# State space layer: the feed-forward half starts one loop step earlier, its first chunk through one PSUM bank

## The chip, the core and the metric

The kernel runs on one core of a Trainium2 chip. A core has a matrix engine (TensorE, here PE), a vector engine (DVE), an activation engine (ACT) and a general engine (POOL), each working through its own queue of instructions in order; they wait for each other on semaphores. Matrix products land in PSUM, which has banks of 512 fp32 numbers per partition. The metric is the device time of one execution in microseconds (us), lower is better. A measurement of this kernel moves by a few tenths of a per cent from run to run: the three runs below lie from 1214.46 to 1218.0 us.

## What is computed

Four transformer-like layers run over 64 images of 36 tokens with 128 features. The change touches the second layer alone: a Mamba-2 state space block followed by a feed-forward block, cut here to what matters.

```python
t = tgt + _mamba2(tgt, ...)           # conv, silu, decay matrix, gated output, W_out
t = _layernorm(t, n1_g, n1_b)
h = jax.nn.gelu(t @ ffn_w1 + ffn_b1, approximate=False) @ ffn_w2 + ffn_b2
return _layernorm(t + h, n3_g, n3_b)  # added to h of the layer below, then normalised again
```

In the state space block `exp` makes the decays between tokens and `tanh` makes the two silu functions; the feed-forward block uses `gelu`. So ACT needs one table of functions in the first block and another in the second.

## The kernel before

**Tiling.** Tokens lie in G = 22 groups of P = 108 (three images of 36). The feed-forward block takes them in nb = 6 chunks (CHUNKS): five of four groups, one of two. In `state_phase`, after some preparation, every engine runs the same loop `for t in range(last)`, whose step t holds a piece of several groups at once, the later stages of earlier groups: `group(t, k)` is group t - k, or nothing.

**The state space stages of a group g**, by step: at t = g DVE writes `ss_cum` (L2646). At t = g+1 PE makes the decay sums (L2465), turns the conv output (L2473, L2474, bank 3) and makes the gate z (L2476, bank 1); ACT takes `exp` (L2560, `ss_L`), copies bank 3 (L2565, `ss_xc`) and takes `tanh` of z (L2568); DVE waits for `ss_xc` at L2658. At g+2 PE multiplies by the values (L2490), DVE makes `ss_ys` and `ss_yz` (L2677, L2679), ACT squares it (L2581). At g+3 PE turns `ss_yz` (L2481), ACT copies it to `ss_yT` (L2572), PE applies W_out (L2498) and DVE adds and takes statistics (L2686 to L2692). At g+4 the group is normalised (DVE L2670, POOL L2381 to L2385). At g+5 PE turns it (L2504) and ACT copies it to `XP` (L2584); at g+6 DVE writes the low part of `XP` (L2653), for the split products. While tiles of the convolution are left (t up to 19), PE and ACT also work on one of them in each step, in bank 2.

**The feed-forward stages**, class `FeedForward`: at every step t from `first_fed` on, each engine appends to its loop step the feed-forward step s = t - `first_fed`. There are `steps` = nb + 4 = 10 of them. With chunk n:
- s = n: `up(n)` on PE: four groups of three products into `hid_bank(i)`, i = 4n + c (L2144); ACT takes `gelu` of each into `fs_hid` (L2216).
- s = n+1: `down(n)` on PE, 16 products (L2160).
- s = n+2: DVE adds it to `T` (L2248) and takes statistics, POOL makes scale and shift (L2117 to L2122), ACT normalises `T`, as the last thing of its step (L2199).
- s = n+3: DVE (L2256, L2259) adds into `H` and takes statistics, POOL again.
- s = n+4: ACT normalises into `XN` (L2199), PE turns it (L2172), ACT copies (L2221), PE makes the routing products (L2182).

Before, `first_fed` = G = 22, so `up(0)` stands in step 22, where the last group (21) has its first PE stage, and `last` is 32. `hid_bank` goes round three banks: 2, 3 and the first of `quad_bank`. Banks 3 and that one are used by the loop until group 21 has been read out of them at step 22; therefore `up(0)` waits for `xc_ready` = G and `decay` = G. `up` lets PE run two `gelu` behind: before product group i it waits for `hid_ready` = i - 2.

**What sets the order** is the order in which the code is written, for each engine, and the semaphores. There is no scheduler. When the loop is over, `logits` (L2266) ends the phase, and the next phase starts behind a barrier.

Of the kernel before, what the change touches and what calls it, by code (L numbers as in the profile page):

```python
# [10 lines left out]
ALU = mybir.AluOpType  # L11
# [9 lines left out]
P = TB * S  # L21
G = -(-BATCH // TB)
# [30 lines left out]
def at_least(eng, sem, value):  # L53

    if not isinstance(value, int) or value > 0:
        eng.wait_ge(sem, value)
# [1999 lines left out]
class FeedForward:  # L2056
# [6 lines left out]
    def __init__(self, nc, m, ctx, sem, io, rows, layer):  # L2063
        sb = lambda s, shape, dt=F32: ctx.enter_context(nc.sbuf_tensor(f"fs_{s}", shape, dt))
        self.m, self.io, self.rows, self.layer = m, io, rows, layer
        self.nb, hid_n = len(CHUNKS), 4 * 128
        self.steps = self.nb + 4
        self.w1_loaded, self.loaded = sem("fs_w1_loaded"), sem("fs_loaded")
        self.w_high, self.w_split = sem("fs_w_high"), sem("fs_w_split")
        self.moved = sem("fs_moved")  # L2070
        self.hid_psum, self.hid_ready, self.y_psum, self.t_sum = sem("fs_hid_psum"), sem("fs_hid_ready"), sem("fs_y_psum"), sem("fs_t_sum")
        self.t_stats, self.t_steps, self.t_rstd = sem("fs_t_stats"), sem("fs_t_steps"), sem("fs_t_rstd")
        self.t_normed, self.t_scaled = sem("fs_t_normed"), sem("fs_t_scaled")
        self.h_sum, self.h_stats, self.h_steps, self.h_rstd = sem("fs_h_sum"), sem("fs_h_stats"), sem("fs_h_steps"), sem("fs_h_rstd")
        self.xn_ready, self.xt_psum, self.xt_ready = sem("fs_xn_ready"), sem("fs_xt_psum"), sem("fs_xt_ready")
        self.lg_psum, self.lg_ready = sem("fs_lg_psum"), sem("fs_lg_ready")
        self.rows_stored = m.kept.enter_context(nc.semaphore("fs_rows_stored"))
        self.w1s, self.w2s = sb("w1s", [128, hid_n]), sb("w2s", [128, hid_n])
        self.b1s, self.wr = sb("b1s", [128, 4]), sb("wr", [128, 8])
        self.w1p = sb("w1p", [128, 2, hid_n], F32R)  # L2080
        self.hid = sb("hid", [128, 2, 4, QUAD * P])
        self.t_bn, self.h_bn = sb("t_bn", [P, G, 6]), sb("h_bn", [P, G, 6])
        self.t_mv, self.h_mv = sb("t_mv", [P, G, 2]), sb("h_mv", [P, G, 2])
        self.t_scale, self.h_scale = sb("t_scale", [P, G]), sb("h_scale", [P, G])
        self.t_shift, self.h_shift = sb("t_shift", [P, G]), sb("h_shift", [P, G])
        self.wide = lambda row, k: m.row(row).unsqueeze(1).broadcast_to([P, k, D])
        self.hid_bank = lambda i: (m.bank[2], m.bank[3], m.quad_bank[:, 0, :])[i % 3]
        self.y_bank = lambda n: (m.bank[1], m.quad_bank[:, 1, :])[n % 2]
        self.turn_bank, self.lg_bank = m.bank[0], m.quad_bank[:, 2, :]

# [40 lines left out]
    def up(self, pe, n):  # L2131
        m, layer = self.m, self.layer
        c0, k = CHUNKS[n]
        pe.wait_ge(layer.t_split, c0 + k)
        if n == 0:
            pe.wait_ge(self.w_split, 1)
            pe.wait_ge(layer.cv_ready, 4 * self.nb)
            pe.wait_ge(layer.xc_ready, G)
            pe.wait_ge(layer.decay, G)
        for c in range(4):  # L2140
            i = n * 4 + c
            at_least(pe, self.hid_ready, i - 2)
            for a, b in PARTS:
                mm = pe.matmul(self.hid_bank(i)[:, 0:k * P], self.w1p[:, a, c * 128:(c + 1) * 128],  # L2144
                               m.XP[:, b, c0 * P:(c0 + k) * P], start=((a, b) == PARTS[0]), stop=((a, b) == PARTS[-1]))
            mm.then_inc(self.hid_psum, 1)
# [124 lines left out]
def state_phase(nc, m, io, taps, rows):  # L2271
# [2 lines left out]


    nb = len(CHUNKS)
    first_fed = G
    with ExitStack() as ctx:
        sem = ctx.enter_context(semaphores(nc, m, "ss"))
        sb = lambda s, shape, dt=F32: ctx.enter_context(nc.sbuf_tensor(f"ss_{s}", shape, dt))  # L2280
# [16 lines left out]
        t_psum, t_ready, t_split = sem("t_psum"), sem("t_ready"), sem("t_split")  # L2297
# [291 lines left out]
        def _(dve):  # L2589
# [43 lines left out]
            for k in (15, 13, 11, 9, 7, 5, 3):  # L2633
# [4 lines left out]
            then(dve.scalar_tensor_tensor(out=m.DTA[:, :].rearrange("p (g e) -> p g e", e=8), in0=m.DT[:, :].rearrange("p (g e) -> p g e", e=8),  # L2638
                                          scalar=-1.0, in1=a_exp[:, :].unsqueeze(1).broadcast_to([P, G, 8]), op0=ALU.mult, op1=ALU.mult))

            for t in range(last):
                if t and (at := tile(t - 1)) is not None:
                    gated(*at)
# [4 lines left out]
                if t == 0:  # L2648
                    for c in range(4):
                        gated(0, c)  # L2650
                if (g := group(t, 6)) is not None:
                    dve.wait_ge(t_ready, g + 1)
                    dve.tensor_tensor(m.XP[:, 1, g * P:(g + 1) * P], t_bank[:, 0:P], m.XP[:, 0, g * P:(g + 1) * P],  # L2653
                                      ALU.subtract).then_inc(t_split, 1)
                if (g := group(t, 1)) is not None:
                    dve.wait_ge(xc_ready, g + 1)
                    at_least(dve, mix_ready, g)
# [35 lines left out]
                if G + 1 <= t < G + 4:  # L2693
                    for n in range(2):
                        feed.move(dve, 2 * (t - G - 1) + n)
                if t >= first_fed:
                    feed.vector(dve, t - first_fed)
            feed.logits(dve)
# [712 lines left out]
```

## Time and profile before

| | us |
|---|---|
| median of 3 runs | 1216.21 |
| lowest, highest | 1214.46, 1218.0 |
| the profiled execution, its own time | 1212.65 |
| its span in the trace | 1210.9 |
| the stretch from step 22 on PE to the last routing product's sum | 511.4 to 576.9 |

The profiled execution is 3.56 us shorter than the median of the runs, and 1.75 us of it lie outside the span. Times in the trace are counted from the start of the span. In a timeline a row begins with the start and the duration of a run of like instructions; what stands in brackets is how long the engine sat idle before it and who released it. Each step of the loop can be found by its rows: `ss_cum` opens PE's part, `XP` ends ACT's part of the loop, `fs_w1p` and `fs_w2s` are `up` and `down`.

### The profile page before, as it was taken

What the parts mean: (1) busy time and instruction counts of PE and PEld (TensorE: products, weight loads), DVE (VectorE), ACT (ScalarE), POOL (GpSimd) and SP (SyncE); (2) the same over time, 40 slices, a digit from 0 to 9 for tenths busy, and PEclk for the clock granted to TensorE, in tenths of its full rate; (3) what the DMA queues carried; (4) which work ended last, traced back from release to release, by engine and by line L of the source; (5) the groups of instructions that cost most, each with busy time, mean ns of one, the idle gap of its engine ahead of it and who ended that gap; (6) DMA issues with size and microseconds to landing.
All of it is one profiled execution on the core that took longest, in us unless ns stands there. A gap on an engine that the chain in (4) does not pass through costs nothing. (4 is left out here: it accounts for less than half of the span.)

```text
span 1210.9 us, 29369 instructions
## 1 busy us (share of the span) xinstructions
PE 1083.4 (89%) x8538; PEld 906.9 (75%) x8538; DVE 926.1 (76%) x2799; ACT 856.6 (71%) x2831; POOL 527.4 (44%) x869
## 2 busy tenths in 40 slices
PE   8899999999998999887397689997899899869996
PEld 7788868888887888786387577786688688657884
DVE  5588868999875889856675797885899788755774
ACT  5598979888885555456253578886788499746995
POOL 0489984445104278865252643223432111034552
PEclk9999989999999999998599799999999999959998
DMA  7300003312110000001522200000443000024441
GB/s 299 98 2 3 2 2 94 97 66 66 61 41 24 1 2 1 2 1 41 199 64 48 68 9 6 7 2 1 133 119 109 21 2 2 3 82 123 130 129 44
DMA packets 50824, 66.68 MB, mean 55 GB/s; under 512 B 8100, under 2 KB 30904, under 8 KB 50552
## 3 DMA queue, kind: packets, MB, share of 16 engines
q1 hardware_dynamic: 44552, 53.39, 14.5%
q0 software_dynamic: 4432, 6.59, 2.1%
q10 hardware_dynamic: 1696, 4.98, 1.0%
q8 instruction: 65, 1.06, 0.4%
q14 instruction: 79, 0.65, 0.2%
HBM read 58.32 MB, written 6.71 MB: 54 GB/s over the span
## 5 line engine op out<-in xcount | busy, mean ns | idle before, releaser
L545 DVE TENSOR_TENSOR f_parts<-T,f_parts 128x512 fp32r<-128x512 f32 (+1 forms) x240 | 185.1, 810 | 21.6 <-ACT f_parts L529 19.7
L521 ACT ACTIVATE T<-quad_bank,f_b1s 128x512 f32<-128x512 f32 (+1 forms) x240 | 150.7, 648 | 47.7 <-PE quad_bank L492 39.0
L492 PE MATMUL quad_bank<-XP,f_wp 128*128 128x512 f32 (+1 forms) x720 | 167.9, 378 | 0.2 <-ACT T L521 0.2
L492 PEld LDWEIGHTS quad_bank<-XP,f_wp 128*128 128x128 f32 x720 | 127.2, 191 | 25.6 <-issue 0.9
L529 ACT ACTIVATE f_parts<-T 128x512 fp32r<-128x512 f32 (+1 forms) x240 | 132.2, 591 | 0.0
L1015 ACT ACTIVATE a_late<-quad_bank,a_shift 108x108 f32<-108x108 f32 x352 | 119.0, 361 | 2.7 <-DVE a_shift L1101 2.6
L505 PE MATMUL bank<-f_parts,f_wp 128*128 128x512 f32 (+1 forms) x480 | 113.7, 372 | 4.6 <-DVE XT L554 2.0
L505 PEld LDWEIGHTS bank<-f_parts,f_wp 128*128 128x128 f32 x480 | 84.0, 188 | 22.4 <-DVE XT L554 2.6
L434 POOL TENSOR_TENSOR f_wp<-f_ws,const 128x512 fp32r<-128x512 f32 (+1 forms) x32 | 34.0, 1064 | 120.5 <-DMA f_ws<-in_f_w 56.0
L1015 ACT ACTIVATION_READ_ACCUMULATOR a_late<-quad_bank,a_shift 108x1 f32 x352 | 76.7, 218 | 0.0
L821 POOL TENSOR_TENSOR a_ve<-a_mv,const 108x1 f32<-108x1 f32 x44 | 8.4, 191 | 148.4 <-DVE a_mv L1158 148.4
L1471 ACT ACTIVATE a_late<-a_masked,a_shift 108x108 f32<-108x108 f32 x176 | 65.1, 374 | 0.8 <-DVE a_shift L1555 0.7
L510 PE MATMUL bank<-f_parts,f_wp 128*128 128x512 f32 (+1 forms) x240 | 63.1, 370 | 0.6 <-DVE f_parts L545 0.6
L3108 ACT ACTIVATE a_E<-quad_bank,a_shift 108x108 f32<-108x108 f32 x184 | 61.9, 353 | 0.7 <-DVE a_shift L3149 0.4
L1097 DVE TENSOR_REDUCE a_mx<-quad_bank 108x4 f32<-108x432 f32 x88 | 53.0, 603 | 9.4 <-PE quad_bank L898 8.3
L1937 ACT ACTIVATE f_hid<-quad_bank,f_b1t 128x128 f32<-128x128 f32 x100 | 28.8, 368 | 41.2 <-PE quad_bank L1905 41.2
L2428 PE MATMUL bank<-ss_xp,ss_wtp 128*128 128x432 f32 (+1 forms) x264 | 55.5, 360 | 2.4 <-ACT ss_th L2527 1.3
L898 PE MATMUL quad_bank<-a_qk 19*108 19x108 f32 x704 | 55.4, 273 | 2.5 <-ACT a_late L1015 1.2
L898 PEld LDWEIGHTS quad_bank<-a_qk 19*108 19x108 f32 x704 | 40.8, 168 | 16.1 <-issue 5.3
L1007 ACT ACTIVATE a_late<-bank 108x432 f32<-108x432 f32 x88 | 48.0, 545 | 4.9 <-PE bank L873 3.2
L574 DVE SCALAR_TENSOR_TENSOR a_late<-bank,f_b2s,a_late 128x512 f32<-128x512 f32 (+1 forms) x70 | 48.1, 687 | 4.2 <-DMA a_late<-f_gates 3.0
L2428 PEld LDWEIGHTS bank<-ss_xp,ss_wtp 128*128 128x128 f32 x264 | 45.5, 191 | 6.1 <-issue 2.9
(484 smaller groups left out, 3119.8 us busy)
## 6 DMA issues: line engine op xcount, KB each, us to landing
a_late<-f_gates SPq DMA_DIRECT2D x64, 256.0 KB, 3.3
a_wqk<-in_a_wqk SPq DMA_DIRECT2D x24, 256.0 KB, 2.5
f_ws<-in_f_w SPq DMA_DIRECT2D x16, 256.0 KB, 4.0
pats<-in_patches SPq DMA_DIRECT2D x5, 648.0 KB, 10.7
pats<-in_patches ACTq DMA_DIRECT2D x5, 648.0 KB, 15.8
a_late<-f_gates SPq DMA_DIRECT2D x16, 128.0 KB, 3.7
f_w1a<-in_f_w SPq DMA_DIRECT2D x1, 2048.0 KB, 10.7
f_w2a<-in_f_w SPq DMA_DIRECT2D x1, 2048.0 KB, 15.5
```

What stands on the lines that cost most here:

```text
L492: mm = pe.matmul(self.m.quad_bank[:, q % 4, 0:w], self.wp[0][:, e % 2, a, c * 128:(c + 1) * 128], self.xp[:, b, t0:t0 + w], start=((a, b) ...
L505: pe.matmul(self.y_bank(i)[:, 0:w], self.wp[1][:, e % 2, a, c * 128:(c + 1) * 128], self.hi[:, q % self.ring, 0:w], start=(c == 0 and a == ...
L510: mm = pe.matmul(self.y_bank(i)[:, 0:w], self.wp[1][:, e % 2, 0, c * 128:(c + 1) * 128], self.lo[:, q % self.ring, 0:w], start=False, stop ...
L521: act.activation(self.full[:, q % 4, 0:w], self.m.quad_bank[:, q % 4, 0:w], self.func, bias=self.b1s[:, e * self.chunks + c:e * self.chunk ...
L529: act.activation(self.hi[:, q % self.ring, 0:w], self.full[:, q % 4, 0:w], ACT.Copy).then_inc(self.hid_high, 1)
L545: dve.tensor_tensor(self.lo[:, q % self.ring, 0:w], self.full[:, q % 4, 0:w], self.hi[:, q % self.ring, 0:w], ALU.subtract).then_inc(self. ...
L898: mm = pe.matmul(sbank[0:P, b, tile * P:(tile + 1) * P], qk[row * b:row * b + used, q, tile, :], qk[row * b:row * b + used, q, tiles + til ...
L1015: e = act.activation(E[:, q, n, :], scores[:, n // tiles, n % tiles, :], ACT.Exp, scale=w.scale, bias=shift[:, q, n:n + 1], accum_out=tota ...
L1097: dve.tensor_reduce(top.rearrange("p (b s) -> p b s", s=tiles), scores[:, banks * half:banks * (half + 1), :, :], AX, ALU.max).then_inc(ma ...
L1471: e = act.activation(E[:, g % 2, n, :], masked[:, half, i, :], ACT.Exp, scale=-1.0, bias=shift[:, g % 2, n:n + 1], accum_out=total[:, g % ...
L2428: mm = pe.matmul(conv_bank(s, c)[:, 0:k * P], wtp[:, a, tap, c * 128:(c + 1) * 128], xp[:, s % 2, b, 0:k * TB, tap:tap + S], start=(tap == ...
L3108: e = act.activation(E[:, u, n, :], scores[:, n // tiles, n % tiles, :], ACT.Exp, scale=scale, bias=shift[:, u, n:n + 1], accum_out=total[ ...
```

## The change

- `first_fed` becomes G - 1 = 21. Every feed-forward step stands one loop step earlier, and `last` becomes 31: the loop has one step fewer.
- `up(0)` now stands in step 21, when banks 3 and `quad_bank` 0 are still wanted by group 21. So its four product groups all go to bank 2, the bank of the convolution, free since step 19: `hid_bank(i)` is bank 2 for i up to 3, and each group waits for the `gelu` of the one before (`hid_ready` = i).
- The wait for `xc_ready` and `decay` moves from `up(0)` to `up(1)`.
- `up(5)` needs the low part of `XP` of group 21, which was written at step 27, and now would come after its reader; it is written at step G + 4 = 26, just before DVE's feed-forward step (`turned_low`).

```diff
-        self.hid_bank = lambda i: (m.bank[2], m.bank[3], m.quad_bank[:, 0, :])[i % 3]
+        self.hid_bank = lambda i: (m.bank[2], m.bank[3], m.quad_bank[:, 0, :])[i % 3 if i > 3 else 0]
...
         if n == 0:
             pe.wait_ge(self.w_split, 1)
             pe.wait_ge(layer.cv_ready, 4 * self.nb)
+        if n == 1:
             pe.wait_ge(layer.xc_ready, G)
             pe.wait_ge(layer.decay, G)
         for c in range(4):
             i = n * 4 + c
-            at_least(pe, self.hid_ready, i - 2)
+            at_least(pe, self.hid_ready, i if n == 0 else i - 2)
...
-    first_fed = G
+    first_fed = G - 1
...
+            def turned_low(g):
+                dve.wait_ge(t_ready, g + 1)
+                dve.tensor_tensor(m.XP[:, 1, g * P:(g + 1) * P], t_bank[:, 0:P], m.XP[:, 0, g * P:(g + 1) * P],
+                                  ALU.subtract).then_inc(t_split, 1)
+
...
-                if (g := group(t, 6)) is not None:
-                    dve.wait_ge(t_ready, g + 1)
-                    dve.tensor_tensor(m.XP[:, 1, g * P:(g + 1) * P], t_bank[:, 0:P], m.XP[:, 0, g * P:(g + 1) * P],
-                                      ALU.subtract).then_inc(t_split, 1)
+                if (g := group(t, 6)) is not None and g < G - 1:
+                    turned_low(g)
...
+                if t == G + 4:
+                    turned_low(G - 1)
                 if t >= first_fed:
                     feed.vector(dve, t - first_fed)
```

No instruction of the computation is added or taken away; the instructions of the changed kernel stand one line lower than before (L2145 for L2144 and so on), from the feed-forward class on.

**PE, from the last row of step 21.** Before, the last group's first stages follow, and then `up(0)` over three banks:

```order
L2504 MATMUL quad_bank<-const,ss_tt 128x108
L2465 MATMUL quad_bank<-ss_cum,const 108x432
L2473 MATMUL bank3<-const,ss_sx 108x128 x2
L2474 MATMUL bank3<-ss_sx 108x108
L2476 MATMUL bank1<-ss_win,XT 108x256
L2481 MATMUL bank0<-const,ss_yz 128x108 x2
L2490 MATMUL quad_bank<-ss_xdt,ss_M 108x64 x4
L2498 MATMUL quad_bank<-ss_wout,ss_yT 108x128 x2
L2504 MATMUL quad_bank<-const,ss_tt 128x108
L2144 MATMUL bank2<-XP,fs_w1p 128x432 x3
L2144 MATMUL bank3<-XP,fs_w1p 128x432 x3
L2144 MATMUL quad_bank<-XP,fs_w1p 128x432 x3
```

Now `up(0)` comes first, twelve products into bank 2, and `up(1)` stands where `up(0)` stood:

```order
L2505 MATMUL quad_bank<-const,ss_tt 128x108
L2145 MATMUL bank2<-XP,fs_w1p 128x432 x12
L2466 MATMUL quad_bank<-ss_cum,const 108x432
L2474 MATMUL bank3<-const,ss_sx 108x128 x2
L2475 MATMUL bank3<-ss_sx 108x108
L2477 MATMUL bank1<-ss_win,XT 108x256
L2482 MATMUL bank0<-const,ss_yz 128x108 x2
L2491 MATMUL quad_bank<-ss_xdt,ss_M 108x64 x4
L2499 MATMUL quad_bank<-ss_wout,ss_yT 108x128 x2
L2505 MATMUL quad_bank<-const,ss_tt 128x108
L2145 MATMUL bank3<-XP,fs_w1p 128x432 x3
```

What moved is `up(0)`, ahead of the eight rows of step 22.

**ACT, from the last row of step 21.** Before, the last `exp` and `tanh` are over when `gelu` begins, and there is one load of a function table:

```order
L2584 ACTIVATE XP<-quad_bank 128x108
L2560 ACTIVATE ss_L<-quad_bank 108x432
L2565 ACTIVATE ss_xc<-bank3 108x364
L2568 ACTIVATE ss_zs<-bank1 108x256
L2572 ACTIVATE ss_yT<-bank0 128x216
L2581 ACTIVATE ss_sq,ss_ssq<-ss_yz 108x256
L2584 ACTIVATE XP<-quad_bank 128x108
L2216 ACT_TABLE_LOAD
L2216 ACTIVATE fs_hid<-bank2,fs_b1s 128x432
L2216 ACTIVATE fs_hid<-bank3,fs_b1s 128x432
```

Now `gelu` of chunk 0 stands ahead of them, and there are three loads:

```order
L2585 ACTIVATE XP<-quad_bank 128x108
L2217 ACT_TABLE_LOAD
L2217 ACTIVATE fs_hid<-bank2,fs_b1s 128x432 x4
L2561 ACT_TABLE_LOAD
L2561 ACTIVATE ss_L<-quad_bank 108x432
L2566 ACTIVATE ss_xc<-bank3 108x364
L2569 ACTIVATE ss_zs<-bank1 108x256
L2573 ACTIVATE ss_yT<-bank0 128x216
L2582 ACTIVATE ss_sq,ss_ssq<-ss_yz 108x256
L2585 ACTIVATE XP<-quad_bank 128x108
L2217 ACT_TABLE_LOAD
L2217 ACTIVATE fs_hid<-bank3,fs_b1s 128x432
```

What moved is the chunk's `gelu`, and a load stands on either side of the loop's part of step 22.

**ACT at step 24**, where the last group's `ss_yT` is copied. Before, the copy comes before the first normalisation of `T` (L2199):

```order
L2572 ACTIVATE ss_yT<-bank0 128x216
L2584 ACTIVATE XP<-quad_bank 128x108
L2216 ACTIVATE fs_hid<-quad_bank,fs_b1s 128x432
L2216 ACTIVATE fs_hid<-bank2,fs_b1s 128x432
L2216 ACTIVATE fs_hid<-bank3,fs_b1s 128x432
L2216 ACTIVATE fs_hid<-quad_bank,fs_b1s 128x432
L2199 ACTIVATE T<-T,fs_t_shift,fs_t_scale 108x128 x4
```

Now it comes behind it:

```order
L2217 ACTIVATE fs_hid<-quad_bank,fs_b1s 128x432
L2217 ACTIVATE fs_hid<-bank2,fs_b1s 128x432
L2217 ACTIVATE fs_hid<-bank3,fs_b1s 128x432
L2217 ACTIVATE fs_hid<-quad_bank,fs_b1s 128x432
L2200 ACTIVATE T<-T,fs_t_shift,fs_t_scale 108x128 x4
L2573 ACTIVATE ss_yT<-bank0 128x216
L2585 ACTIVATE XP<-quad_bank 128x108
```

The normalisation of the first chunk has moved from the end of step 24 to the end of step 23, ahead of the copy.

## Rows read from the trace of the kernel before

**Rows 1.** The page: the span.

```profile
span 1210.9 us, 29369 instructions
```

**Rows 2.** Stretches: start:end, length, busy time of each engine, granted clock (PEclk).

```profile
526.70:558.50 31.80, 29.42 (x237) 28.08 (x236) 19.24 (x78) 20.11 (x48) 17.45 (x34) 1.00 0.06 15
558.50:577.00 18.50, 10.24 (x67) 8.88 (x65) 10.08 (x41) 10.46 (x26) 9.59 (x23) 0.71 0.16 42
```

**Rows 3.** The timeline of PE, steps 21 to 25 and on: start, duration, operation.

```profile
511.31 0.26 PE L2504 MATMUL quad_bank<-const,ss_tt 108*128 108x108 f32 x1
511.40 1.51 PE L2465 MATMUL quad_bank<-ss_cum,const 108*108 108x432 f32 x2
...
513.14 0.56 PE L2474 MATMUL bank<-ss_sx 128*108 128x108 f32 x2
...
516.05 1.43 PE L2144 MATMUL bank<-XP,fs_w1p 128*128 128x432 f32 x6
...
520.59 0.86 PE L2144 MATMUL bank<-XP,fs_w1p 128*128 128x432 f32 x3 [2.51 <-ACT fs_hid L2216]
...
523.57 1.43 PE L2144 MATMUL bank<-XP,fs_w1p 128*128 128x432 f32 x3
...
526.74 3.65 PE L2160 MATMUL bank<-fs_w2s,fs_hid 128*108 128x128 f32 x32
...
531.02 0.69 PE L2498 MATMUL quad_bank<-ss_wout,ss_yT 128*108 128x128 f32 x4 [0.44 <-ACT ss_yT L2572]
...
534.02 3.65 PE L2160 MATMUL quad_bank<-fs_w2s,fs_hid 128*108 128x128 f32 x32
...
541.58 3.65 PE L2160 MATMUL bank<-fs_w2s,fs_hid 128*108 128x128 f32 x32
...
548.79 3.66 PE L2160 MATMUL quad_bank<-fs_w2s,fs_hid 128*108 128x128 f32 x32
...
554.88 3.66 PE L2160 MATMUL bank<-fs_w2s,fs_hid 128*108 128x128 f32 x32
```

**Rows 4.** The timeline of ACT around the table load, and of its first normalisations.

```profile
513.86 0.24 ACT L2584 ACTIVATE XP<-quad_bank 128x108 fp32r<-128x108 f32 x1
...
514.41 0.48 ACT L2565 ACTIVATE ss_xc<-bank 108x364 f32<-108x364 f32 x1
...
518.63 1.28 ACT L2216 ACT_TABLE_LOAD   x1
...
520.94 0.62 ACT L2216 ACTIVATE fs_hid<-quad_bank,fs_b1s 128x432 f32<-128x432 f32 x1
...
538.54 1.65 ACT L2199 ACTIVATE T<-T,fs_t_shift,fs_t_scale 108x128 f32<-108x128 f32 x4 [3.69 <-POOL fs_t_shift L2122]
...
547.07 0.60 ACT L2216 ACTIVATE fs_hid<-bank,fs_b1s 128x432 f32<-128x432 f32 x1
```

**Rows 5.** The timeline of DVE at step 22, step 25 and the end of the phase.

```profile
514.92 0.27 DVE L2658 TENSOR_TENSOR ss_cbm<-ss_xc,const 108x108 f32<-108x108 f32 x1 [0.49 <-ACT ss_xc L2565]
...
524.61 1.26 DVE L2230 TENSOR_TENSOR H<-H,rows 108x512 f32<-108x512 f32 x2
...
533.79 0.68 DVE L2248 TENSOR_TENSOR T<-T,bank 108x512 f32<-108x512 f32 x1
...
545.35 0.69 DVE L2248 TENSOR_TENSOR T<-T,bank 108x512 f32<-108x512 f32 x1 [2.12 <-PE bank L2160]
...
549.98 0.23 DVE L2653 TENSOR_TENSOR XP<-quad_bank,XP 128x108 fp32r<-128x108 f32 x1
...
576.56 0.34 DVE L2266 TENSOR_TENSOR LG<-quad_bank,rows 108x176 f32<-108x176 f32 x1 [5.52 <-PE quad_bank L2182]
```

**Rows 6.** Stretches of PE alone, 1 us long: busy time, granted clock.

```profile
510.00:511.00 1.00, 0.22 (x2) 1.00 0.00 0
...
512.00:513.00 1.00, 1.00 (x4) 0.50 0.00 0
```

**Rows 7.** Who waited for whom on PE from 511 to 577 us: total, times, longest.

```profile
PE bank L2144 <- ACT fs_hid L2216: 4.5, 3, 2.5
```

## Prediction

> **What bounds the kernel now.** I read the stretches first, then PE's waits, then the timelines. From `down(0)` to the end of `down(4)` PE is busy for 29.42 of 31.80 us at a granted clock of 1.00 [rows 2]: this stretch is PE's own work, nearly back to back. What follows `down(4)` is a chain of sums, normalisations and turns in which PE is busy 10.24 of 18.50 us [rows 2]; it ends with `logits` at 576.56 [rows 5], and nothing of the next phase can start before. So the end of the phase is the start of `down(4)`, 554.88, plus a tail of 21.7 us whose order the change leaves alone. The reader needs five landmarks on PE, the starts of `down(0)` to `down(4)`: 526.74, 534.02, 541.58, 548.79, 554.88 [rows 3]. There is one visible thing to win: within `up(0)` PE sat idle 2.51 us for the first `gelu` [rows 3], out of 4.5 us of such waits in the phase [rows 7]. There is one fact against it: ACT is not free for a `gelu` before its last work of step 21 ends at 513.86 + 0.24 = 514.10, and the table load costs 1.28 us more [rows 4]. One step fewer is worth nothing in itself, since no instruction goes away; it is worth what idle time it removes.
>
> **Step 21: `up(0)` through one bank.** PE reaches it at 511.3 [rows 3] and runs its first group at once. `gelu` 0 can start at 514.10 + 1.28 = 515.4 and takes 0.62 [rows 4]: done at 516.0. Each of the other three groups then waits for the `gelu` before it. A group takes 0.86 us at the full clock and 1.43 at half [rows 3], both clocks occurring, 1.00 and 0.50 [rows 6], a `gelu` 0.62, and a hand-over 0.05 (`ss_xc` ends at 514.89 and its reader starts at 514.92 [rows 4, 5]; I round up). That is 1.6 or 2.15 us a round. The clock fell to 0.50 in 512 to 513 after a microsecond in which PE was busy only 0.22 [rows 6]; here PE idles over 3 us before the second group, so I take the full clock for one round and half for two. The last group starts at 519.8 and PE is free at 521.0. At the full clock throughout it would be 519.9. Before, the same PE was already in step 22 at 511.40 [rows 3].
>
> **Step 22: two more table loads.** ACT ends the fourth `gelu` at 521.9. `exp` and `tanh` of group 21 need the other table: 1.28 us, then `ss_L` (0.4) and `ss_xc` (0.48 [rows 4]), done at 524.1 where it was 514.9. PE had its input ready at 521.0 + 2.3 = 523.3 (511.40 to 513.14 + 0.56 [rows 3]), so ACT decides. DVE's part of the step shifts by 9.2 us with it. From DVE's reader of `ss_xc` to the start of ACT's load it was 514.92 to 518.63 [rows 4, 5], 3.7 us; I take 3.5, as the shift leaves POOL time to be ready. So the third load begins at 527.6, the first `gelu` of chunk 1 ends at 529.5, and the fourth group of `up(1)`, which waits for it, lets `down(0)` start at 530.4 instead of 526.74: **+3.7**. The two loads (2.6 us) are inside this sum, one fully exposed, the other behind PE's groups.
>
> The Trainium skill (ScalarE: Activation LUTs, What ACT_TABLE_LOAD costs) puts every switch of set at about 1.28 us of load and 1.38 us of drain; its section Table sets: the hidden batching unit asks to batch calls by set, which speaks against this change. The trace agrees on the load and not on the drain. By the page's price the two added loads would cost some 2.8 us more, and the forecast would be +12.7.
>
> **Step 23.** From `down(0)` to `down(1)` took 7.3 us [rows 3]. Now the value product of group 21 lies in it too; I take 7.6: `down(1)` at 538.0, **+4.0** in all.
>
> **Step 24: the last group behind the first normalisation.** DVE can add chunk 0 into `T` only after its own part of step 23, which waits for the output product of group 20 (ends near 535.9), then statistics (0.9) and two `H` additions (1.2 [rows 5]): 538.0. From there to ACT's normalisation took 533.79 to 538.54, 4.75 us [rows 4, 5]: it starts at 542.8 and ends at 544.4. Before, ACT had copied `ss_yT` of group 21 ahead of it, and PE waited 0.44 us [rows 3]. Now the copy is behind it, and PE, which is there at 541.9, starts the output product only at 544.75: 2.8 us idle. From that product to the next `down` it took 3.0 us [rows 3]; `down(2)` starts at 547.8, **+6.2**.
>
> **Step 25: DVE late, then ACT.** DVE gets group 21's sum at 545.4, and after the same 2.1 us adds chunk 1 into `T` at 547.5. That addition to the low part of `XP` took 545.35 to 549.98 [rows 5], 4.6 us: 552.2. PE needs it to turn group 20 and is free at 551.3: 1.1 us idle. ACT normalises `T` at 547.5 + 4.75 = 552.2, then `XN` (1.65 each [rows 4]), so its first `gelu` of chunk 4 comes at 555.6 instead of 547.07 [rows 4]. `down(3)` came 1.72 us behind that: 557.3, **+8.5**.
>
> **Step 26: the moved low part.** PE turns group 21 at 561.5, ACT copies it (0.24), DVE makes the low part (0.23), and `up(5)`, which before stood right behind, waits for both, about 0.9 us in all. ACT's normalisation of `XN` can only begin after that copy, and `gelu` behind it costs another 0.5. `down(4)`: 6.1 + 1.4 us after `down(3)`, 564.8, **+9.9**. The tail hangs on it unchanged. DVE waits for the copy of group 21 at its `turned_low`, with chunk 3's sum queued behind; that is inside the same 9.9. POOL's queue is only later with DVE's, and SP stores `XN` chunk by chunk behind it.
>
> **The sum.** Against the profiled execution 1212.65 + 9.9 = 1222.6 (its span 1210.9 [rows 1] + 9.9 = 1220.8). Against the median of the runs, 3.56 us higher: 1216.21 + 9.9 = 1226.1, or 0.8% slower.
>
> **Bounds of what the trace doesn't show.** The clock after so many short waits: at full clock throughout, 1.1 less (8.8). If half the clock also catches `down(0)`, its 3.65 us double: 3.5 more; another 2 if it catches a later chunk. In the tail PE did idle and the clock was 0.71 on average [rows 2], so this can happen. A later wait can turn out shorter than worked out: the 2.8 us of step 24 can vanish if DVE and POOL serve chunk 0 faster, and steps 25 and 26 can be absorbed in part. Then about +4 is left.
>
> **Rivals.**
> 1. *The later waits are absorbed.* Steps 21 to 23 cost what is worked out, but PE takes the rest up: +4, 1220. For it: ACT and DVE have gaps. Against it: the copy of `ss_yT` stands behind the normalisation in ACT's own queue.
> 2. *Half the clock in PE's long stretch*: +9.9 + 3.5 to 5.5, 1229.6 to 1231.6. For it: the clock fell after idling [rows 6]. Against it: after the 2.51 us of idling it was back before `down(0)` (1.00 in 526.70 to 558.50 [rows 2]). The Trainium skill (TensorE: Matmul & The Clock Gate, What's actually happening) has the clock depend on how busy PE has been of late, which bears this rival out in kind.
> 3. *Not slower: the moved chunk fills PE.* `up(0)` runs where PE idled, so the 2.51 us go, and PE keeps the full clock through step 22, which at 0.50 took 4.65 us (511.40 to 516.05 [rows 3, 6]) and would take some 3.2: together -4, 1212.2. It decides by ACT: `gelu` 0 would have to end about when PE's second group could start, 512.4, and ACT is busy until 514.10 without the load. Only if DVE, not PE, set the pace of all that follows would the delay be hidden.
> 4. *The page's drain*: +12.7, 1228.9.
> 5. *Nothing happens*, the delays of steps 21 and 22 cancelled by fewer waits later (4.5 us in all to be had [rows 7]): within 0.3%.
>
> **Chances.** Forecast as worked out (+7.5 to +12.5) 0.55; rival 1 0.17; rival 2 0.12; rival 3 0.04; rival 4 0.03; rival 5 0.09. A measurement can tell 0.3%, 3.6 us, from no change. Rival 1 sits just above this bound, and I count a third of it (0.05) as no change. Faster 0.04, same 0.14, slower 0.82. The range takes in rivals 1, 2 and 4: 1219.5 to 1232.
>
> **What would show it.** In the trace of the changed kernel: three table loads between 514 and 529 us; `up(0)` with three waits of PE for `gelu`; PE idle over 2 us before the output product of group 21, released by the copy of `ss_yT`; the five landmarks at 530.4, 538.0, 547.8, 557.3, 564.8; `logits` at 586.5. The prediction is wrong if `down(0)` starts by 527, or if the landmarks stop drifting after `down(1)`, which is rival 1, or if the granted clock falls below 1.00 in that stretch, rival 2.

## The result

The changed kernel is slower: 1227.22 us (median of 4 runs, 1225.51 to 1228.42) against 1216.87 us for the kernel before in the same comparison. The ratio is 1.0094, with a 95% interval of 1.0069 to 1.0119. The forecast was 1226.1 us. In a second comparison, 1227.73 against 1215.47 us, the ratio was 1.0096 (1.0069 to 1.0124). So the change costs 0.9 to 1.0%; the medians differ by 10.4 and 12.3 us, and the two intervals together reach from 8.4 to 15 us.

To compare traces I measure one stretch, called D: from PE's turn of group 16, the last thing that both kernels do in the same place, to the start of `logits`. Before, D is 576.56 - 511.31 = 65.25 [rows 3, 5].

### The profile page after: what moved, and what is told of

It is laid out like the page before. It is cut to its first block and busy times, and to the rows that moved or that the text cites. A ratio compares the mean times of both kernels' runs of the same rounds, so it can differ in the third digit from the quotient of the medians.

```text
span 1226.0 us, 29371 instructions
## 1 busy us (share of the span) xinstructions
PE 1090.5 (89%) x8538; PEld 912.4 (74%) x8538; DVE 924.9 (75%) x2799; ACT 858.4 (70%) x2833; POOL 521.5 (43%) x869
## 5 line engine op out<-in xcount | busy, mean ns | idle before, releaser
L505 PE MATMUL bank<-f_parts,f_wp 128*128 128x512 f32 (+1 forms) x480 | 115.6, 377 | 4.0 <-DVE a_late L574 1.7
L505 PEld LDWEIGHTS bank<-f_parts,f_wp 128*128 128x128 f32 x480 | 85.1, 190 | 22.1 <-DVE a_late L574 2.6
L434 POOL TENSOR_TENSOR f_wp<-f_ws,const 128x512 fp32r<-128x512 f32 (+1 forms) x32 | 31.3, 978 | 125.8 <-DMA f_ws<-in_f_w 64.7
L510 PE MATMUL bank<-f_parts,f_wp 128*128 128x512 f32 (+1 forms) x240 | 64.2, 376 | 0.1
L510 PEld LDWEIGHTS bank<-f_parts,f_wp 128*128 128x128 f32 x240 | 43.7, 191 | 8.9 <-DVE f_parts L545 0.7
```

The source lines that it names most:

```text
L505: pe.matmul(self.y_bank(i)[:, 0:w], self.wp[1][:, e % 2, a, c * 128:(c + 1) * 128], self.hi[:, q % self.ring, 0:w], start=(c == 0 and a == ...
L510: mm = pe.matmul(self.y_bank(i)[:, 0:w], self.wp[1][:, e % 2, 0, c * 128:(c + 1) * 128], self.lo[:, q % self.ring, 0:w], start=False, stop ...
```

## The profile after

The page of the changed kernel, its span and the busy time of its engines:

```profile
span 1226.0 us, 29371 instructions
PE 1090.5 (89%) x8538; PEld 912.4 (74%) x8538; DVE 924.9 (75%) x2799; ACT 858.4 (70%) x2833; POOL 521.5 (43%) x869
```

As many products as before, and two more ACT instructions: the table loads. The timeline of PE in the changed kernel (start, duration, operation, idle before and releaser), which answers to [rows 3]:

```profile
511.73 0.26 PE L2505 MATMUL quad_bank<-const,ss_tt 108*128 108x108 f32 x1
511.76 0.83 PE L2145 MATMUL bank<-XP,fs_w1p 128*128 128x432 f32 x3
516.51 1.45 PE L2145 MATMUL bank<-XP,fs_w1p 128*128 128x432 f32 x3 [3.91 <-ACT fs_hid L2217]
518.67 1.45 PE L2145 MATMUL bank<-XP,fs_w1p 128*128 128x432 f32 x3 [0.71 <-ACT fs_hid L2217]
...
530.38 0.90 PE L2145 MATMUL bank<-XP,fs_w1p 128*128 128x432 f32 x3 [2.11 <-ACT fs_hid L2217]
531.08 5.30 PE L2161 MATMUL bank<-fs_w2s,fs_hid 128*108 128x128 f32 x32
...
540.17 3.65 PE L2161 MATMUL quad_bank<-fs_w2s,fs_hid 128*108 128x128 f32 x32
...
546.01 0.69 PE L2499 MATMUL quad_bank<-ss_wout,ss_yT 128*108 128x128 f32 x4 [2.00 <-ACT ss_yT L2573]
...
549.01 3.65 PE L2161 MATMUL bank<-fs_w2s,fs_hid 128*108 128x128 f32 x32
553.74 0.28 PE L2505 MATMUL quad_bank<-const,ss_tt 108*128 108x108 f32 x1 [1.07 <-issue]
...
558.38 1.45 PE L2145 MATMUL bank<-XP,fs_w1p 128*128 128x432 f32 x3 [2.40 <-ACT fs_hid L2217]
...
560.34 4.36 PE L2161 MATMUL quad_bank<-fs_w2s,fs_hid 128*108 128x128 f32 x32
...
566.17 0.59 PE L2145 MATMUL quad_bank<-XP,fs_w1p 128*128 128x216 f32 x3 [0.65 <-DVE XP L2644]
...
568.53 3.66 PE L2161 MATMUL bank<-fs_w2s,fs_hid 128*108 128x128 f32 x32
```

`up(0)` has its three waits, the last group's output product waits 2.00 us for the copy behind the normalisation, and the moved low part holds `up(5)` back for 0.65 us. ACT in the same stretch, answering to [rows 4]:

```profile
514.28 0.24 ACT L2585 ACTIVATE XP<-quad_bank 128x108 fp32r<-128x108 f32 x1
514.54 1.28 ACT L2217 ACT_TABLE_LOAD   x1
515.84 0.62 ACT L2217 ACTIVATE fs_hid<-bank,fs_b1s 128x432 f32<-128x432 f32 x1
...
522.95 1.28 ACT L2561 ACT_TABLE_LOAD   x1
...
528.41 1.28 ACT L2217 ACT_TABLE_LOAD   x1
...
544.08 1.65 ACT L2200 ACTIVATE T<-T,fs_t_shift,fs_t_scale 108x128 f32<-108x128 f32 x4 [3.09 <-POOL fs_t_shift L2122]
545.63 0.33 ACT L2573 ACTIVATE ss_yT<-bank 128x216 f32<-128x216 f32 x1
```

And two rows of DVE. The first had waited for `ss_xc` of group 21, which ACT makes only behind the chunk's four `gelu` and the second table load; the other row ends the phase:

```profile
525.17 0.27 DVE L2662 TENSOR_TENSOR ss_cbm<-ss_xc,const 108x108 f32<-108x108 f32 x1 [10.32 <-ACT ss_xc L2566]
...
590.67 0.34 DVE L2267 TENSOR_TENSOR LG<-quad_bank,rows 108x176 f32<-108x176 f32 x1 [5.98 <-PE quad_bank L2183]
```

D is now 590.67 - 511.73 = 78.94: 13.7 us more than before, where the forecast had 9.9. The granted clock tells most of why. Stretches of the changed kernel, as in [rows 2]:

```profile
514.00:524.00 10.00, 6.07 (x14) 3.79 (x15) 0.73 (x4) 5.33 (x9) 2.56 (x7) 0.50 0.00 0
524.00:531.00 7.00, 4.89 (x32) 4.27 (x32) 3.69 (x12) 4.87 (x12) 3.39 (x8) 0.98 0.00 0
531.00:534.00 3.00, 3.00 (x16) 2.96 (x15) 0.05 (x1) 0.94 (x2) 1.36 (x3) 0.51 0.03 5
```

PE ran at 1.2 GHz (0.50) for ten microseconds around `up(0)`, and again for the first three of `down(0)`, which took 5.30 us where it took 3.65 before.

Who waited for whom on PE, the changed kernel, 511 to 590 us, answering to [rows 7]:

```profile
PE bank L2145 <- ACT fs_hid L2217: 9.9, 5, 3.9
...
PE quad_bank L2499 <- ACT ss_yT L2573: 2.8, 2, 2.0
```

The change was to remove some of PE's waits for `gelu`, 4.5 us in all before [rows 7]; they have grown to 9.9.

## The experiments

Each was compared with the kernel before on the chip on which it ran. "Before, again", "changed, again", "one table" and "one bank" ran on one chip, "copy first", "kept busy", "changed, mended" and "early load" on a second, and the two with "and busy" on a third, so two ratios of different chips are compared with less certainty than two of one. D is from one profiled execution each. The columns "down" have the start of that product group counted from the turn of group 16. Several causes act on the same microseconds (a round of `up(0)` is longer both by its wait and by the clock), so the shares found below overlap and can't be added up.

| kernel | ratio to before (95%) | D | down(0) | down(2) | down(4) |
|---|---|---|---|---|---|
| before | | 65.25 | 15.43 | 30.27 | 43.57 |
| before, again | 1.0005 (0.9988 to 1.0022) | 64.36 | 14.09 | 28.93 | 42.23 |
| changed | 1.0094 (1.0069 to 1.0119) | 78.94 | 19.35 | 37.28 | 56.80 |
| changed, again | 1.0096 (1.0069 to 1.0124) | 78.53 | 19.35 | 37.30 | 56.85 |
| one table | 1.0069 (1.0042 to 1.0096) | 76.40 | 17.20 | 35.15 | 54.73 |
| one bank | 1.0038 (1.0022 to 1.0055) | 70.19 | 20.38 | 35.21 | 48.52 |
| copy first | 1.0095 (1.0070 to 1.0119) | 75.34 | 19.35 | 34.05 | 53.66 |
| kept busy | 1.0075 (1.0054 to 1.0096) | 73.46 | 17.58 | 35.29 | 51.78 |
| changed, mended | 1.0069 (1.0046 to 1.0093) | 70.25 | 15.92 | 30.64 | 48.57 |
| mended and busy | 1.0040 (1.0023 to 1.0058) | 70.72 | 14.72 | 29.43 | 49.05 |
| early load | 0.9983 (0.9966 to 1.0000) | 62.51 | 12.71 | 27.54 | 40.84 |
| early and busy | 0.9986 (0.9971 to 1.0001) | 62.51 | 12.71 | 27.54 | 40.83 |

### Both kernels once more

> The kernel before, unchanged, once more. Measure for all runs: D, from PE's turn of group 16 (the last row of step 21's loop part; 511.31 in the first profile) to the start of logits (576.56): 65.3 us before, 590.67 - 511.73 = 78.9 after, so +13.7 inside the phase in one profile each, while the medians differ by 10.4. Theory 1 (the phase is repeatable, and the rest of the gap lies in other phases of single executions): D = 65.3 within 0.5, ratio 1.000 within 0.002. Rival (the phase itself varies by microseconds with the clock): D differs by more than 1.

> The changed kernel, unchanged, once more. Theory 1: D = 78.9 within 0.5 and down(0) again at half clock in part (5.3 us against 3.65). Rival (how much of the phase runs at half clock is chance): D between 75.2, the 9.9 forecast, and 79, with down(0) at 3.65 us when it is short. Ratio to before 1.008 to 1.012 by both.

The changed kernel repeated itself to 0.4 us, half clock in `down(0)` (5.32 us) included. The kernel before did so less well: D is 0.9 us shorter, which meets neither the 0.5 us of theory 1 nor the more than 1 of its rival. The table shows where: `down(0)` comes 1.34 us sooner, and of this the stretch behind `down(4)` gives 0.45 back. The 1.34 us lie in step 23. Stretches of PE alone, the first profile and then the repeat:

```profile
522.00:523.00 1.00, 1.00 (x7) 0.50 0.00 0
523.00:524.00 1.00, 1.00 (x6) 0.50 0.00 0
```

```profile
512.00:514.00 2.00, 1.56 (x12) 1.00 0.00 0
...
522.00:524.00 2.00, 2.00 (x14) 1.00 0.01 4
```

The first profile was also at 0.50 from 512 to 513 [rows 6], where the repeat has 1.00, but this cost nothing: from `ss_cum` to `up(0)` it took 4.65 us in the one and 4.60 in the other, since at the full clock PE waits there for ACT and DVE instead (0.83 and 0.33 us). In the tail it was the repeat that fell sooner:

```profile
559.17 3.12 PE L2160 MATMUL quad_bank<-fs_w2s,fs_hid 128*108 128x128 f32 x16
```

This `down(5)` took 1.91 us in the first profile. So when the clock falls, in a phase that idles now and then, differs from execution to execution, and moved D by about 1 us here. The cost of the change in D is 13.7 us against the first profile and 14.2 between the two repeats. Both lie within the intervals of the ratios (8.4 to 15 us). Other phases of a span also differ by a microsecond or two between profiles, which is why I judge single terms by D.

### One table

Edit: chunk 0 takes a function that lies in the same table as `exp`.

```diff
-                act.activation(self.hid[:, s % 2, c, 0:k * P], self.hid_bank(i)[:, 0:k * P], ACT.Gelu,
+                act.activation(self.hid[:, s % 2, c, 0:k * P], self.hid_bank(i)[:, 0:k * P], ACT.Gelu if s else ACT.Tanh,
```

> The changed kernel with tanh instead of gelu for chunk 0 of the feed-forward block (this part of the computation is replaced): chunk 0 needs no other function table, so one load of three is left. Theory 1 (the two added loads are exposed on PE's path in steps 21 and 22): first activation of chunk 0 1.28 us sooner, ss_xc of group 21 2.6 us sooner, down(0) 2.4 to 2.6 sooner, D = 76.3, ratio to before 1.0065 to 1.0085. Rival A (the loads hide behind PE's groups): D = 78 to 79. Rival B (the clock is what costs, and shorter idling keeps it up): D below 74.5.

D is 76.40, 2.1 to 2.5 us less than in the two profiles of the changed kernel, and `down(0)` is 2.15 us sooner. ACT in this kernel:

```profile
511.39 0.24 ACT L2585 ACTIVATE XP<-quad_bank 128x108 fp32r<-128x108 f32 x1
511.53 0.61 ACT L2217 ACTIVATE fs_hid<-bank,fs_b1s 128x432 f32<-128x432 f32 x1
513.09 0.62 ACT L2217 ACTIVATE fs_hid<-bank,fs_b1s 128x432 f32<-128x432 f32 x1 [0.94 <-PE bank L2145]
...
517.41 0.62 ACT L2217 ACTIVATE fs_hid<-bank,fs_b1s 128x432 f32<-128x432 f32 x1 [1.54 <-PE bank L2145]
518.85 0.53 ACT L2561 ACTIVATE ss_L<-quad_bank 108x432 f32<-108x432 f32 x1 [0.82 <-PE quad_bank L2466]
```

And PE's second group, which ran at the full clock here and at half in the changed kernel (1.45 us):

```profile
512.20 0.85 PE L2145 MATMUL bank<-XP,fs_w1p 128*128 128x432 f32 x3 [2.49 <-ACT fs_hid L2217]
```

Counted from the turn of group 16, the first activation of chunk 0 starts 1.42 us sooner than in the changed kernel: this is the first load with the gaps beside it, fully exposed. The fourth starts 2.02 us sooner, since one of the three rounds took 1.56 us and not 2.16: that is the clock. `ss_L` starts 2.51 us sooner, so the second load was worth only 0.5 us more: without it ACT waits 0.82 us for PE's `ss_cum` product, a wait that the load had covered. Of these 2.51 us `down(0)` keeps 2.15, where 2.4 to 2.6 were expected. So at `ss_L` the two added loads make 1.9 us, and the clock 0.6. Theory 1 is right in D (76.3 expected) and in the ratio, but it took both loads for exposed, and the second was so for less than half. Rival A, with D at 78 to 79, falls, though it holds in part for the second load. Rival B falls too, with D below 74.5: only one round came back to the full clock, and `down(0)` took 5.32 us as before.

### One bank

Edit: the kernel before, `first_fed` 22, with these lines of the change alone.

```diff
-        self.hid_bank = lambda i: (m.bank[2], m.bank[3], m.quad_bank[:, 0, :])[i % 3]
+        self.hid_bank = lambda i: (m.bank[2], m.bank[3], m.quad_bank[:, 0, :])[i % 3 if i > 3 else 0]
...
-            at_least(pe, self.hid_ready, i - 2)
+            at_least(pe, self.hid_ready, i if n == 0 else i - 2)
```

> The kernel before with one part of the change alone: first_fed stays 22, one table load, but the four groups of up(0) go through bank 2, each waiting for the gelu before it. Theory 1 (serial groups cost PE a round of 1.6 to 2.15 us for each of the two that used to run ahead): the last group of up(0) starts 3.2 to 4.3 us later than 520.59, down(0) 3 to 4 us later, D = 68.5 to 69.5, ratio 1.002 to 1.004. Rival (ACT, not PE, sets the pace here, since it ends the four gelus at 522.1 anyway): D = 66 to 67.

The ratio, 1.0038, is as theory 1 had it; D is 70.19, more than the 68.5 to 69.5 that it had: 4.9 us over the first profile of before, 5.8 over the repeat. PE in this kernel:

```profile
516.48 0.83 PE L2144 MATMUL bank<-XP,fs_w1p 128*128 128x432 f32 x3
521.05 1.45 PE L2144 MATMUL bank<-XP,fs_w1p 128*128 128x432 f32 x3 [3.74 <-ACT fs_hid L2216]
523.22 1.45 PE L2144 MATMUL bank<-XP,fs_w1p 128*128 128x432 f32 x3 [0.71 <-ACT fs_hid L2216]
525.38 1.45 PE L2144 MATMUL bank<-XP,fs_w1p 128*128 128x432 f32 x3 [0.71 <-ACT fs_hid L2216]
```

All three rounds run at half clock, 2.16 us each, and so does step 23 behind them (its clock is 0.50 up to 530 us). From the turn of group 16 to the last group it is 4.3 us more than before, the upper end of theory 1; what is beyond it is step 23 at half clock. One bank instead of three costs by itself over a third of what the change costs, before anything is moved. This share has the half clock that the waits bring with them in it, so it overlaps with the clock's share below.

### The copy first

Edit: at the end of step 23 ACT makes the copy of group 21 before it normalises `T`, and no longer at the start of step 24.

```diff
+        if s == 2:
+            self.before_norm()
         if 0 <= s - 2 < nb:
             self.norm(act, s - 2, m.T[0:P, :], m.T[0:P, :], self.t_scale, self.t_shift, self.t_rstd, self.t_normed)
...
-                if (g := group(t, 3)) is not None:
+                if (g := group(t, 3)) is not None and g < G - 1:
+                    turned_copy(g)
```

> The changed kernel with one pair of ACT's instructions exchanged: the copy of ss_yT of group 21 stands ahead of the first normalisation of T, at the end of step 23. D is the time from PE's turn of group 16 to the start of logits (65.3 before, 78.9 after). Theory 1 (the 2.00 us that PE idles before the output product of group 21 come from this order and pass on to the end): PE idle there 0.4, down(2) 1.6 sooner, D = 77.0 to 77.5. Rival (the chain of sums and normalisations on DVE, POOL and ACT sets steps 24 and 25 anyway): down(2) sooner, D = 78.5 to 79.

PE's idle time at the output product is 0.44 us instead of 2.00, and from `down(1)` to `down(2)` it is 7.27 us instead of 8.84, 1.6 less. PE in this kernel:

```profile
532.71 3.65 PE L2161 MATMUL bank<-fs_w2s,fs_hid 128*108 128x128 f32 x32
...
544.42 0.69 PE L2501 MATMUL quad_bank<-ss_wout,ss_yT 128*108 128x128 f32 x4 [0.44 <-ACT ss_yT L2562]
```

D fell by 3.2 to 3.6, more than the 1.4 to 1.9 expected, because `down(0)`, which starts at the same 19.35, ran at the full clock this time (3.65 us and not 5.30). Up to there the two kernels run the same instructions, so this second part isn't the edit's but the execution's. The time does not show the gain: the ratio is 1.0095. The span fell by nothing either, since in this execution the rest of the program took longer (638.0 us behind `logits` against 635.3 and 635.8 in the changed kernel's two). So the order's 1.6 us is seen in the trace and not confirmed by the times, which can't tell it.

### PE kept busy

Edit: products on constants, whose results nothing reads, in the gaps.

```diff
             mm.then_inc(self.hid_psum, 1)
+            if n == 0 and c < 3:
+                at_least(pe, layer.decay, G - 1)
+                keep_busy(pe, m, m.quad_bank[:, 0, :], (9, 1, 1)[c])
+            if n == 1 and c == 2:
+                keep_busy(pe, m, m.bank[0], 4)
```

> The changed kernel with products on constants, whose results are not used, in PE's gaps: nine after the first group of up(0), one after the second and third, four in up(1) ahead of its last group. Theory 2 (part of the cost is half clock after idling: the groups of up(0) took 1.45 us instead of 0.83, down(0) 5.30 instead of 3.65): granted clock 1.00 from 514 to 536, groups 0.85, down(0) 3.65, D = 75.5 to 76.5. Rival (ACT's loads and gelus cover it): D = 78 to 79.

D is 73.46, 5.1 to 5.5 us less than the changed kernel, where 2.4 to 3.4 were expected, and the ratio is 1.0075. PE in this kernel, and two stretches of PE alone:

```profile
512.00 4.05 PE L66 MATMUL quad_bank<-const 128*128 128x256 f32 x18
...
528.85 3.65 PE L2166 MATMUL bank<-fs_w2s,fs_hid 128*108 128x128 f32 x32
```

```profile
514.00:518.00 4.00, 3.71 (x17) 1.00 0.00 0
...
542.00:546.00 4.00, 3.87 (x16) 0.67 0.01 4
```

The clock stays at 1.00 to 542 us, the rounds take 1.57 us instead of 2.16, and `down(0)` takes 3.65. Two counts agree on what the half clock is worth in the changed kernel. Between the starts of `down(0)` to `down(4)` in the table, the filler gains 1.8 us up to `down(0)` and 5.0 up to `down(4)`. And the changed kernel's own rows give the same: 1.8 in three rounds, 1.65 in `down(0)`, 0.9 in the group before `down(3)` and the turns with it, 0.7 in `down(3)`. On the way the filler kernel lost 1.4 us in step 24, where PE idled 2.01 us for the copy as before and the clock then fell (0.67 in 542 to 546), and won this back in step 25, whose waits for DVE and ACT shrank by it. So about 5 of the 14 us in D are the clock's. The times agree in direction only: 1.0075 and 1.0094 to 1.0096 have intervals that overlap, and are from two chips.

What remains is 9.1 us against the repeat of before, and up to `down(4)` 8.2 us against the first profile and 9.6 against the repeat. The forecast's sum for the full clock was 8.8.

### Three repairs, and with the filler as well

Edits: "changed, mended" has the exchanged copy, and in steps 21 and 22 a `gelu` of one column of constants where ACT idles, which brings the table load with it (the lines of this second edit are below). "Mended and busy" has also five, one and one filler products between the groups of `up(0)`.

```diff
+                if t in (G - 1, G):
+                    act.activation(early[:, t % 2:t % 2 + 1], m.eps[0:P, :], ACT.Gelu)
                 if (at := tile(t)) is not None:
                     evict(*at)
```

> The changed kernel with the exchanged copy of ss_yT and with gelu of one column of constants in steps 21 and 22, in ACT's idle time, so that two of three table loads lie there. Theory 1: first gelu of chunk 0 at the end of step 21's XP copy (1.3 sooner), first gelu of chunk 1 1.3 sooner, PE's idle time at the output product 0.4: D = 74 to 75, still some 9 us over before. Rival (the step sooner wins once the loads are out of the way): D at or below 65.3.

> The changed kernel with the exchanged copy, the two early table loads and products on constants (results not used) between the groups of up(0), five after the first and one after the second and third. With the loads, the order and the clock out of the way only the structure is left: four serial groups in step 21 and the later steps on DVE, ACT and POOL. Theory 1: granted clock 1.00 in steps 21 and 22, D = 68.0 to 69.3 against 64.4 of the repeat of the kernel before, which had the full clock as well; ratio to before 1.003 to 1.007. Rival (the three repairs together bring the change to even): D = 65.5 or less, ratio 1.000 or less.

Both are still slower than the kernel before, by 0.7% and 0.4%, with both intervals above 1. So the rivals, that the step sooner would then be worth something or break even, both fall. In D they are at 70.25 and 70.72, where 74 to 75 and 68.0 to 69.3 were expected. The first did better than expected, since `down(0)` and `down(3)` kept the full clock. The second gained another 1.2 us up to `down(2)` and lost it in `down(3)`, which fell to half clock behind a wait of PE for `gelu` of chunk 4; its expectation had the clock out of the way. For "mended and busy", who waited for whom on PE (total, times, longest), and the stretch of PE alone in which the clock fell:

```profile
PE bank L2145 <- ACT fs_hid L2220: 4.0, 5, 2.4
...
PE quad_bank L2511 <- issue: 1.1, 1, 1.1
PE quad_bank L2145 <- DVE XP L2655: 0.7, 1, 0.7
```

```profile
552.00:556.00 4.00, 4.00 (x24) 0.57 0.15 42
```

The three waits that no repair touched (2.4 us for `gelu` behind two normalisations, 1.1 for DVE's low part of group 19, 0.7 for the low part of group 21) are 4.2 us together; the kernel before had 0.6 us of wait in the same place. The trace names no releaser for the 1.1 us ("issue"). That it is the low part of group 19 I take from the semaphore in the code, and from the changed kernel's trace, where this low part ends at 553.64 and PE's turn starts at 553.74. `down(2)` of "mended and busy" is at 29.43, between the 28.93 and 30.27 of before: up to there the repaired schedule loses at most 0.5 us. The rest comes behind it, from those three waits and the half clock of `down(3)` (5.26 us instead of 3.65).

### The kernel before with its load early

Edit: the same line as above, in the kernel before, in step 22 alone; the second kernel has two filler products as well.

```diff
+                if t in (G,):
+                    act.activation(early[:, t % 2:t % 2 + 1], m.eps[0:P, :], ACT.Gelu)
```

> The kernel before with one more ACT instruction, gelu of one column of constants in step 22, after the copy of ss_yT, where ACT sat idle 2.55 us: the table load moves there with it. Theory 1 (the load lies on the path: PE waited 2.51 us for the first gelu): PE's wait 1.2 us, D = 64.0, ratio 0.999. Rival (the waits behind it take the gain up): D = 65.3.

> The kernel before with the early table load in step 22 and two products on constants (results not used) in PE's wait ahead of the last group of up(0). Theory 1: the early load alone is worth 1.3 to 1.9 us of D and the filler only guards the clock, which was 1.00 there in the profile with the early load: D = 62.0 to 62.8, ratio 0.998. Rival (the gain of the early load was a matter of the clock): D = 64.4 or more, ratio 1.000.

ACT and PE in the kernel with the early load:

```profile
514.13 1.28 ACT L2575 ACT_TABLE_LOAD   x1
...
517.21 1.12 ACT L2216 ACTIVATE fs_hid<-bank,fs_b1s 128x432 f32<-128x432 f32 x2
```

```profile
517.88 0.86 PE L2144 MATMUL bank<-XP,fs_w1p 128*128 128x432 f32 x3 [1.16 <-ACT fs_hid L2216]
```

PE's wait is 1.16 us instead of 2.51 or 2.57, and D is 62.51 in both kernels, 1.9 us less than the repeat of before. Only 1.4 of these are the load's: `down(0)` and `down(4)` both come 1.4 us sooner than in the repeat, which had the full clock up to there as well. The other 0.5 us lie in the tail, where `down(5)` kept the full clock and took 1.91 us, against 3.12 in the repeat:

```profile
557.21 1.91 PE L2160 MATMUL quad_bank<-fs_w2s,fs_hid 128*108 128x128 f32 x16
```

The clock in steps 22 and 23 was at 1.00 with and without the filler, so the 1.4 us aren't the clock's. In time the two kernels are faster by 0.17 and 0.14%, which is 2.1 and 1.7 us, each at the edge of its interval (up to 1.0000 and 1.0001). Neither alone is clear of no change; that the two agree, and agree with the trace, speaks for a real gain of 1.4 us or a little more. It is the only version here that is not slower than the kernel before.

## Why the prediction was right, and where its terms were off

The direction and the mechanism of every step held, and the time came within the range of the forecast as worked out. The phase itself grew by more than that: 13.7 us in D where 9.9 were forecast, with +7.5 to +12.5 around them. This is within what rival 2 had, half the clock in PE's long stretch, +13.4 to +15.4. Landmarks, counted from the turn of group 16 (forecast, measured): `down(0)` 19.1, 19.35; `down(1)` 26.7, 28.44; `down(2)` 36.5, 37.28; `down(3)` 46.0, 48.61; `down(4)` 53.5, 56.80; `logits` 75.2, 78.94.

- **Step 21.** The three rounds came as worked out, only that all three ran at half clock and not two: 0.6 us more.
- **Step 22.** Three loads of 1.28 us at 514.54, 522.95 and 528.41, the first of the two added ones fully exposed and the other for 0.5 us, much as the forecast had it ("one table"). `down(0)` came 3.9 us later than before, forecast 3.7; against the repeat of before, which had the full clock in step 23, it is 5.3.
- **Step 23.** This term was too small: 7.6 us were taken, 9.1 measured. `down(0)` ran at half clock for about three microseconds, 5.30 us instead of 3.65. Where it kept the full clock, the step took 7.43 us ("copy first", "kept busy"), so without the clock the 7.6 was right.
- **Step 24.** The order of copy and normalisation did what was said, but the term was too large: PE idled 2.00 us, not 2.8, and the step took 8.8 us and not 9.8. From DVE's addition to ACT's normalisation it was 3.90 us (540.18 to 544.08), not the 4.75 of before; POOL's power of four columns within it took 1.02 us and not 1.85.
- **Step 25.** Too small: 9.5 us taken, 11.3 measured. PE's idle 1.07 at the turn of group 20 was as forecast (1.1). What was missed: POOL made the scale of `T` and then that of `H`, 1.86 us for the power of the second, so ACT's `XN` waited 0.91 us. PE waited 2.40 us for the `gelu` behind it and came back at half clock: from that `gelu` to `down(3)` it took 2.6 us and not 1.72.
- **Step 26.** The term itself was exact. It took 8.2 us where 7.5 were forecast, and the 0.7 is `down(3)` at half clock (4.36 us). With `down(3)` at the full clock the step took 7.49 us ("kept busy", "changed, mended"), 1.4 more than the 6.09 of before.
- **The tail.** It took 22.1 us instead of 21.7 in this profile, and 21.7 in the repeat.

**The signs.** Of what the forecast said would show it, the three loads, the three waits of `up(0)`, PE idle for the copy (2.00 us, where it had said over 2) and landmarks that go on drifting (+3.9, +5.7, +7.0, +11.1, +13.2 against the first profile of before) are there. So is what it named as the sign of rival 2: the granted clock fell below 1.00 in the long stretch (0.51 at 531 to 534).

**The rivals.** Rival 1 fell: the later waits were not absorbed. Rival 2 came true in part, on top of the forecast: its terms were 3.5 us for a doubled `down(0)` and up to 2 for a later chunk, where `down(0)` lost 1.65 and `down(3)` with the group before it 1.6. Rival 3, that the moved chunk fills PE, failed where the forecast said it would be decided: ACT was not free before 514.52. Its price was wrong as well: it put PE's part of step 22, 4.65 us before, at 3.2 for the full clock, and in the repeat of before, at 1.00 throughout, it took 4.60. Rival 4, the drain behind a table load, did not show. The Trainium skill puts a drain of about 1.38 us beside each load (ScalarE: Activation LUTs, What ACT_TABLE_LOAD costs). This trace does not agree: ACT's copy ends at 514.52, the load runs from 514.54 for 1.28 us, and the next function starts at 515.84. Rival 5 falls with the ratio.

**What is luck in it.** Without the clock the forecast's sum was 8.8 us, and 8.2 to 9.6 were measured ("kept busy"); step 24, taken too large by 1.0 us, and step 25, taken too small by as much without its clock, cancel in it. The clock was counted at 1.1 us and cost about 5. That the time was 1227.22 us against a forecast of 1226.1 is in part luck, since the medians of the first comparison differ by 10.4 us where the phase grew by 13.7; in the second they differ by 12.3. The times, with 8.4 to 15 us, can't tell 9.9 from 13.7. What stays open is how the terms of single repairs show in the time: "copy first" has a D shorter by 3 us and no shorter time.

## What to carry to other kernels

A stage that starts a step sooner wins only the idle time that it fills; before moving it, look at which engine's queue it enters and what stands behind it there. Putting work that needs another function table between work that needs the first adds loads, and each costs what the other engines' work doesn't cover: here 1.4 us for one and 0.5 for the other. Where a table must change, a one-column call in an idle gap moves the load there (1.4 us won here). Groups that share one bank wait for each other in short rounds; give them several banks where these are free, and when they can't have them, count the matrix engine's rounds, and the work right behind them, at half clock too.

## What the runs showed of the hardware that I had not expected

- The same kernel at the same place ran once at 0.50 and once at 1.00 of the clock. At 512 to 514 this cost nothing, since PE would have waited; at 522 to 525 it cost 1.3 us. The Trainium skill says of it that the same kernel may be measured with different numbers of slow products (TensorE: Matmul & The Clock Gate, What's actually happening). It tells this of a kernel's start; these traces agree in kind, in the middle of a kernel.
- Through the short waits of a serial chain PE stayed at 0.50 from 514 to 524, and the work behind it paid too. With unused products in the same gaps it ran at 1.00, and D was 5 us shorter ("kept busy").
- POOL's power of 108x4 numbers took 1.02 us in step 23 of the changed kernel, 1.46 in step 24, and 1.86 for `H` right behind that. No run here shows what decides it.
